# A gated attention block: k of two tiles ahead of q at the outset, and small operations moved between VectorE, ScalarE and GpSimd

## What is computed

```python
xn = layernorm(x)
# s: linear attention and a gated feed-forward part
q, k, v = split(xn @ Wqkv + bqkv)
qp, kp = elu(q) + 1, elu(k) + 1
kv = einsum('bsd,bse->bde', kp, v); num = qp @ kv; den = qp . sum(kp)
x1 = layernorm(xn + num / (den + 1e-6)) * g1 + b1
s = layernorm(x1 + (silu(x1 @ Wg + bg) * (x1 @ Wu + bu)) @ Wd + bd) * g2 + b2
# g: three cycles of a coupling network, and a global network on the mean over the tokens
gf = sigmoid(gelu(gelu(mean(xn) @ gc_w1 + b) @ gc_w2 + b) @ gc_w3 + b)
for 3 cycles:
    tf = sigmoid(gelu(gelu(gelu(out @ w1 + b) @ w2 + b) @ w3 + b) @ w4 + b)
    out = out + (0.1 + range * (0.7 * gf + 0.3 * tf - 0.5) * 2) * twist(out)
return x + s * silu(out)
```

## Time and profile before

| | |
|---|---|
| median of 3 runs | 165.39 us (165.28 to 165.51) |
| the profiled execution, its own time | 163.89 us |
| its span, first to last instruction | 162.1 us |
| TensorE clock granted in it, mean | 0.986 of full |
| busy in the span: PE, DVE, ACT, POOL | 94%, 85%, 81%, 72% |

### The profile page before, as it was taken

One profiled execution on the slowest core, in us unless ns is written; L12 is line 12 of the kernel. 1 busy time (PEld: TensorE's weight loads), 2 busy tenths in 40 slices (PEclk: granted clock), 3 DMA queues, 4 the chain that ended last, 5 costly groups with the idle time before them and its releaser, 6 DMA issues.

```text
span 162.1 us, 3409 instructions
## 1 busy us (share of the span) xinstructions
PE 152.6 (94%) x934; PEld 117.0 (72%) x934; DVE 137.4 (85%) x549; ACT 131.6 (81%) x345; POOL 116.9 (72%) x202
## 2 busy tenths in 40 slices
PE   7889999999999899999999999999999999999940
PEld 7567988888888595545554565788888888888840
DVE  2998699899988998299999968978767999978893
ACT  3989796998999978999999986995648985844950
POOL 0078676699981869995089597379999998896573
PEclk9999999999999999999999999999999999999995
DMA  5997333030230000000000000000000110110113
GB/s 172 256 382 167 65 67 69 0 69 19 50 65 0 2 6 0 0 0 4 0 0 0 4 4 0 0 0 4 0 0 7 60 65 6 65 67 0 65 65 129
DMA packets 11923, 7.83 MB, mean 48 GB/s; under 512 B 8961, under 2 KB 9729, under 8 KB 11905
## 3 DMA queue, kind: packets, MB, share of 16 engines
q1 hardware_dynamic: 11472, 7.28, 15.5%
q10 hardware_dynamic: 432, 0.34, 0.6%
HBM read 3.43 MB, written 2.10 MB: 34 GB/s over the span
## 4 chain that ended last, share of the span: by engine, by line
PE 82%; ACT 7%; issue 3%; DMA 2%; DVE 2%; POOL 2%; POOLq 0%; ACTq 0%; DVEq 0%
PE bank L1074 11%; PE bank L1266 10%; PE bank L1191 7%; PE bank L1255 7%; PE bank L1257 7%; PE bank L1256 7%; PE bank L1203 4%; PE bank L1145 4%; PE bank L1216 4%; PE bank L1132 3%; PE bank L1133 3%; PE bank L1136 3%; PE bank L1156 3%; DMA col<-in_cols 2%; PE bank L1281 2%
## 5 line engine op out<-in xcount | busy, mean ns | idle before, releaser
L515 ACT ACTIVATE pq<-bank,bffn 128x512 f32<-128x512 f32 (+1 forms) x24 | 16.1, 682 | 9.3 <-PE bank L1257 9.3
L271 POOL TENSOR_TENSOR rstd<-ve,minus_half 128x4 f32<-128x4 f32 x21 | 21.2, 1011 | 1.7
L816 DVE SCALAR_TENSOR_TENSOR pq<-bank,bffn,pq 128x512 f32<-128x512 f32 (+1 forms) x24 | 17.6, 739 | 5.2 <-issue 2.4
L1255 PE MATMUL bank<-x_hi,ffn_hi 128*128 128x512 f32 (+1 forms) x48 | 20.5, 427 | 0.0
L1256 PE MATMUL bank<-x_lo,ffn_hi 128*128 128x512 f32 (+1 forms) x48 | 18.9, 395 | 0.0
L1257 PE MATMUL bank<-x_hi,ffn_lo 128*128 128x512 f32 (+1 forms) x48 | 18.9, 394 | 0.0
L1266 PEld LDWEIGHTS bank<-wd,pq 128*128 128x128 f32 x144 | 17.9, 191 | 1.3
L1266 PE MATMUL bank<-wd,pq 128*128 128x128 f32 x144 | 18.0, 274 | 0.0
L455 ACT ACTIVATE q_stage<-bank,col 128x512 f32<-128x512 f32 x24 | 16.0, 677 | 0.1
L269 POOL TENSOR_SCALAR nm<-mv 128x4 f32<-128x4 f32 x21 | 4.7, 223 | 15.4 <-DVE mv L653 15.4
L323 POOL TENSOR_TENSOR ab<-cpl 128x8 f32<-128x8 f32 x4 | 9.7, 2426 | 8.1 <-ACT cpl L487 8.0
(11 more groups left out here) (174 smaller groups left out, 457.7 us busy)
## 6 DMA issues: line engine op xcount, KB each, us to landing
x_tok<-in_x SPq DMA_DIRECT2D x8, 256.0 KB, 6.8
tx_tok<-xn_tok SPq DMA_DIRECT2D x16, 128.0 KB, 2.4
out<-pq SPq DMA_DIRECT2D x6, 256.0 KB, 2.0
r_tok<-in_w_ffn SPq DMA_DIRECT2D x1, 341.0 KB, 6.8
r_tok<-in_w_first SPq DMA_DIRECT2D x1, 320.0 KB, 3.5
out<-pq SPq DMA_DIRECT2D x2, 128.0 KB, 1.7
out<-pq ACTq DMA_DIRECT2D x1, 256.0 KB, 2.2
row<-in_rows SPq DMA_DIRECT2D x1, 192.0 KB, 6.3
```

What stands on the lines that cost most here:

```text
L271: return pool.tensor_tensor(rstd[i][:, b], ve[i][:, b], minus_half[:], ALU.pow)
L816: dve.scalar_tensor_tensor(out=hid[b % 2][0:m, c], in0=up_of(n)[0:m], scalar=bffn[0:m, CHUNKS + c:CHUNKS + c + 1], in1=sg[n % 2][0:m], op0 ...
L1255: pe.matmul(dst[0:m], ffn_hi[:, w], x1_hi[:, b], start=True, stop=False)
```

## The change

1. **PE at the outset.** `project_first` replaces `project_q(0)`, `project_tokens(0)` and `project_tokens(1)`: hi·hi of the two tiles first, then q's, then the rest in the order in which the parts are made. `turn_rows` stands ahead of it.
2. **The halves of batch 0.** The high part of its first half is made by DVE (`hi_first_0`), the second by ACT after the wide cast of `first_hi`. DVE makes the wide `first_lo` before `lo_first(0)` and the narrow one after it, and measures all of batch 2 with its moments before its first `feature_k`; `feature_q(0)` stands after two of them. ACT's `exp_q(0)` stands after tile 1.
3. **ACT to POOL.** `centre_sign` is made by POOL, with a semaphore of its own.
4. **DVE to POOL.** `small_columns` (without `bias_rows`, which DVE now does after norming batch 0) and the sums of x-normed (`join_sums`, two instructions for one) run on POOL in pass b = 7 of its loop, the one ahead of `rstd_of(1, 5)` and the other behind `negate_twisted(3, 4, 5)`.
5. **FFN weights.** Their high part (ACT) and low part (DVE) are made in two halves of 341 columns, after tiles 3 and 6 on ACT, after `feature_k` of tile 6 and after batch 1 on DVE.

```diff
@@ gpsimd @@
+            def join_sums():
+
+                pool.wait_ge(sums_ready, 1)
+                pool.wait_ge(xT_hi_ready, BATCHES - 1)
+                pool.wait_ge(xT_lo_ready, BATCHES)
+                link(pool.tensor_scalar(ctx_sum[:], sum_hi, -OFFSET * SEQ, 0.0, ALU.add, ALU.add))
+                pool.tensor_tensor(ctx_sum[:], ctx_sum[:], sum_lo, ALU.add).then_inc(ctx_ready, 1)
+
+            def small_columns():
...
+                pool.tensor_scalar(gain[:, 1:2], col[:, COL["range"]:COL["range"] + 1], W_TOKEN, 0.0,
+                                   ALU.mult, ALU.add).then_inc(cols_ready, 1)
...
+            pool.tensor_scalar(centre_sign, eye, sign[:, 0:1], minus_mean_sign[:, 0:1], ALU.mult,
+                               ALU.add).then_inc(sign_ready, 1)
...
             for b in range(BATCHES + 2):
                 if b + 2 < BATCHES:
                     norm_x(b + 2)
+                if b == BATCHES - 1:
+                    small_columns()
                 if b >= 2:
                     rstd_of(1, b - 2)
...
                 for done in {6: (0, 1, 2), 7: (3, 4, 5), 8: (6,), 9: (7,)}.get(b, ()):
                     negate_twisted(done)
+                if b == BATCHES - 1:
+                    join_sums()
@@ scalar @@
-            act.activation(centre_sign, eye, ACT.Identity, scale=sign[:, 0:1],
-                           bias=minus_mean_sign[:, 0:1]).then_inc(centre_ready, 1)
...
-            hi_first(0)
-            hi_first(1)
             act.wait_ge(w_ps, 2)
             act.copy(first_hi[:, 0:4 * D], ps_w[:]).then_inc(first_hi_ready, 1)
+            hi_first_1()
             for b in range(BATCHES):
-                exp_q(b)
+                if b >= 1:
+                    exp_q(b)
                 for t in range(TILES):
                     token_tile(TILES * b + t)
-                    if t == (1 if b else 2) and b + 1 < BATCHES:
+                    if b == 0 and t == 1:
+                        exp_q(0)
+                    if t == 1 and b + 1 < BATCHES:
                         hi_x(b + 1)
...
+                    if (b, t) in FFN_AFTER:
+                        split_ffn(FFN_AFTER.index((b, t)))
@@ vector @@
+            def hi_first_0():
+                dve.wait_ge(xT0_ps, 1)
+                dve.tensor_scalar(xT_hi[:, 0, 0:2 * P], ps_xT0[0], OFFSET, 0.0, ALU.add, ALU.add,
+                                  accum_out=half_sums[:, 0, 0:1]).then_inc(xT0_hi_ready, 1)
...
             norm_first(0)
+            bias_rows()
...
-                if b == BATCHES - 1:
-                    dve.wait_ge(sums_ready, 1)
-                    dve.wait_ge(xT_lo_ready, BATCHES)
-                    dve.scalar_tensor_tensor(out=ctx_sum[:], in0=sum_hi, scalar=-OFFSET * SEQ, in1=sum_lo,
-                                             op0=ALU.add, op1=ALU.add).then_inc(ctx_ready, 1)
                 if b >= 1:
                     copy_kv(b - 1)
...
+                if b == 1:
+                    ffn_low(0)
@@ tensor @@
+            def project_first():
...
+                for t in range(2):
+                    pe.matmul(ps_k[t][:], hi[t], first_hi[:, wide], start=True, stop=False)
+                pe.wait_ge(xT0_hi1_ready, 1)
+                pe.matmul(ps_q[:], first_hi[:, wq], xT_hi[:, 0], start=True, stop=False)
...
             transpose_first()
+            turn_rows()
+            project_first()
```

More of the change, by code:

```diff
@@ L643, in measure @@
                 last.then_inc(st_ready[i], 1)
-            def measure_part(b, tiles):
-                for t in tiles:
-                    last = dve.bn_stats(st[0][:, b, t], x_tok[:, b, t])
-                return last
             def moments(i, b, tiles=range(TILES), half=0):
@@ L942, in _ @@
             moments(0, 1)
[L943 to L947 removed]
+            hi_first_0()
             dve.wait_ge(first_hi_ready, 2)
@@ L955, in _ @@
                     add_eps(b - 2)
-                feature_q(b)
+                if b >= 1:
+                    feature_q(b)
                 if b >= 2:
@@ L973, in _ @@
                 if b == 0:
-                    small_columns()
+                    feature_q(0)
+                    lo_x(1)
                 if 1 <= b < BATCHES - 1:
@@ L1106, in transpose_x @@
                 transposes(ps_xT, xn_tok[:, b]).then_inc(xT_ps, 1)
-            def project_q(b):
-                if b == 0:
-                    pe.wait_ge(xT0_hi_ready, 2)
-                    pe.wait_ge(first_ready, 1)
-                else:
-                    pe.wait_ge(xT_hi_ready, b)
-                if b >= 1:
-                    pe.wait_ge(qf_ready, b)
+            def project_first():
+                wq, wide = slice(4 * D, 5 * D), slice(0, 4 * D)
+                hi = [xT_hi[:, 0, t * P:(t + 1) * P] for t in range(2)]
+                lo = [xT_lo[:, 0, t * P:(t + 1) * P] for t in range(2)]
+                pe.wait_ge(xT0_hi_ready, 1)
+                pe.wait_ge(first_hi_ready, 2)
+                for t in range(2):
+                    pe.matmul(ps_k[t][:], hi[t], first_hi[:, wide], start=True, stop=False)
+                pe.wait_ge(xT0_hi1_ready, 1)
+                pe.matmul(ps_q[:], first_hi[:, wq], xT_hi[:, 0], start=True, stop=False)
+                pe.wait_ge(first_ready, 1)
+                for t in range(2):
+                    pe.matmul(ps_k[t][:], hi[t], first_lo[:, wide], start=False, stop=False)
+                pe.wait_ge(xT0_lo_ready, 1)
+                for t in range(2):
+                    pe.matmul(ps_k[t][:], lo[t], first_hi[:, wide], start=False, stop=True).then_inc(k_ps, 1)
+                pe.wait_ge(first_ready, 2)
+                pe.matmul(ps_q[:], first_lo[:, wq], xT_hi[:, 0], start=False, stop=False)
+                pe.wait_ge(xT_lo_ready, 1)
+                pe.matmul(ps_q[:], first_hi[:, wq], xT_lo[:, 0], start=False, stop=True).then_inc(q_ps, 1)
+            def project_q(b):
+                pe.wait_ge(xT_hi_ready, b)
+                pe.wait_ge(qf_ready, b)
                 hi, lo = xT_hi[:, b % 2], xT_lo[:, b % 2]
```

92 lines of the change are left out of this document (44 added, 48 removed).

## The result

The changed kernel takes **170.98 us** (median of 4 runs, 169.91 to 171.69); beside it the kernel before took 165.33 (4 runs, 165.28 to 165.51). The ratio is 1.033, 95% interval 1.028 to 1.039: slower, by 5.65 us. The profiled execution took 171.69, with a span of 169.0 where before had 162.1. It is the longest of the four: their spans are 168.0, 168.3, 168.9 and 169.0.

A forecast was written before the change was run, and what follows sets the result against it. PE (TensorE), busy for 94% of the span, was taken to bound the kernel. Outset +0.2, wait for POOL's join +4.8 and cold clock +1.4 made +6.4 us on a median of 165.39: 171.8 us, range 169.9 to 173.7.

The forecast's parts named there:

- part 3: `join_sums` behind POOL's list in pass 7: PE's `global_layer(0)` waits for it and starts 4.8 us later.
- the outset's 0.2: First microseconds, up to batch 1: the new order was to cost +0.2 us, bounds -0.1 and +0.5.
- part 2: Batch 7 on DVE: without `ctx_sum`, up to 0.91 us, the copy of kv starts 0.8 us earlier.
- A gain of some 0.6 us, if nothing else came up: Batch 7: PE's wait of 0.57 us for DVE's copy of kv would go once `ctx_sum` leaves DVE.
- part 4: TensorE's clock after PE's wait for `ctx_ready`: it falls to half and costs 1.4 us.
- The bounds of 0 and 2.5: Price in us of the halved clock behind PE's wait: nothing at one end, 2.5 at the other.
- the rival's argument: Clock full from the first matmul, so its return may be quick; rival: wait without cold clock, 170.4 us, chance 0.20.
- part 1: The outset: PE's first matmul at about 8.65, `feature_k(0)` 0.2 to 0.3 us later, in all +0.2 us.
- the lower bound: The outset at -0.1 us, where `hi_first_0` is short and PE's earlier start comes through.
- 2.12 us "for five steps that it still has": The outset on DVE: time needed from the aggregation at 7.67 to batch 2's statistics at 9.79, kept in full.
- What it loses or wins before 64 us is carried to the end: PE is busy for all of 89.0 us from 64 to 153 us, so no gap there makes good a loss.
- The sum: Whole kernel: +0.2 + 4.8 + 1.4 = +6.4 us, giving 171.8 us, chance 0.67.

The follow-up runs named there:

- busy run: The changed kernel with 20 unused matmuls of the identity on PE ahead of `global_layer(0)`: 168.49 us, ratio 1.025.
- swap run: The kernel before with POOL's `scale_x1(3)` behind the negations of pass 6 instead of ahead of them: 164.29 us, ratio 0.999.
- the early join alone: The kernel before with only `ctx_sum` moved, as `join_sums` on POOL at the start of pass 7: 164.09 us, ratio 0.997.
- move alone: The kernel before with only `ctx_sum` moved off DVE, onto POOL behind `negate_twisted(3, 4, 5)`: 171.47 us, ratio 1.041.
- wait of 2.85: The changed kernel with `join_sums` between `norm_x1(5)` and `scale_x1(4)` of POOL's pass 7: 167.78 us, ratio 1.018.
- the join first: The changed kernel with only `join_sums` moved, to the start of POOL's pass 7: 164.76 us, ratio 1.003.
- the sum on DVE: The changed kernel with `ctx_sum` back on DVE in its old place: 164.21 us, ratio 0.997.
- the scalars on DVE: The changed kernel with `join_sums` at the start of POOL's pass 7 and POOL's `scalars_2` made by three DVE instructions: 163.78 us, ratio 0.996.

## Why the prediction was right, and which steps failed

- **The place of the loss (part 3)** was right. Forecast: POOL at 57.0, 5.99 us of list, `ctx_ready` 63.5, PE at 63.55. Measured: 57.22, 6.01, about 63.8, 63.93. DVE's moments ended at 57.11 and not at 57.0, and `small_columns`, which "fit into its idle time", filled it to 57.14; the join's second instruction started 0.35 behind the first, not 0.28. Behind its end PE took another 0.15 us. The forecast had added the outset's 0.2 apart, so PE was due at 63.75. That the two agree within 0.2 is in part luck: the profiled execution started late, for a reason that the forecast didn't have (see the outset), and in the busy run, where it didn't, PE came at 63.28.
- **DVE's sum (part 2)** was right on DVE: the copy of kv at 54.33 (forecast 54.3), and the swap run shows the reason. "A gain of some 0.6 us, if nothing else came up" isn't settled: `global_layer(0)` moved by 0.24 in the swap run, and with the early join alone the ratio is worth 0.5 at its middle, with an interval of 0.05 to 0.9.
- **The clock (part 4)**: forecast 1.4, measured 1.65 (changed kernel), 1.09 (move alone) and 1.19 (wait of 2.85). The bounds of 0 and 2.5 held. What I had wrong is the moment of the fall, for which I had one row: less than 2 us after PE's last work at the end of the trace of before, and 1.6 to 3.2 us in these runs. And the rival's argument, a clock that is full from the first matmul on, rested on a column that doesn't show the start (see the end).
- **The outset (part 1)** came out at the forecast number for another reason. Forecast: 8.65, 11.60, 14.5; measured 8.84, 11.54, 14.44. But these rows belong to an execution in which the first matmuls ran slow (1.49 us in L1107). Where they took 0.81, the changed outset gave 11.04 to 11.17 and 13.94 to 14.06 (the join first, the sum on DVE, the busy run, the scalars on DVE), and the old one 11.13 to 11.33 and 14.07 to 14.26 (the kernel before, the move alone, the swap): the new one is some 0.2 ahead at the middle, though the ranges touch. PE's first matmul of the projections came at 8.37 to 8.50 there, 0.2 to 0.35 ahead of the kernel before's 8.72, where I had allowed 0.1. So the case that I had put at the lower bound, a short `hi_first_0` and an earlier start that comes through, is what happened. Two terms failed. `hi_first_0` was to be 0.48; it holds DVE for 0.31. And 2.12 us "for five steps that it still has" contained little waits: the aggregation takes 0.30 of it and the other four steps 1.61, not 1.82. DVE's rows from the run with the join first:

```profile
7.62 0.38 DVE L679 BATCH_NORM_AGGREGATE mv<-st 128x2 f32<-128x6 f32 x4
7.92 0.39 DVE L702 TENSOR_SCALAR_CACHE_REDUCE xT_hi<-bank 128x256 fp32r<-128x256 f32 x1
...
9.84 0.87 DVE L673 BATCH_NORM_STATS2 st<-x_tok 128x6 f32<-128x128 f32 x4
...
11.04 0.25 DVE L732 SCALAR_TENSOR_TENSOR kf<-ek,bank 128x128 f32<-128x128 f32 x1
```

  In sum 0.38 less: +0.27 becomes -0.11. With the join back on DVE and everything else of the change in place the medians say -0.3 (interval -0.9 to 0.0), where I had +0.2.
- **"What it loses or wins before 64 us is carried to the end"** was right for the loss and half right for a win: the 0.68 us of the early join were carried to 97 us and lost at 105.
- **The sum**: +6.4 forecast, +5.65 by the medians, +6.9 by the span of the profiled execution (the longest of its four). Its rows give 5.20 + 1.65, where the forecast had 0.2 + 4.8 and 1.4. For the medians the outset has the other sign: with L1261 at 63.28, as in the busy run, and a clock of 1.09 to 1.65, an estimate from these rows is 5.6 to 6.2. What the three executions without rows lost at each place isn't known. So the place and the kind of the loss were forecast; that the total came within 1 us rests in part on an outset of the wrong sign.

## What to carry to other kernels

When an instruction is moved to a less loaded engine, count the list ahead of its new place to the moment when its result is wanted. This one takes 0.46 us on POOL. Behind 6 us of POOL's work it made the kernel before 4.1% slower; at the head of the same pass it cost nothing. In this kernel, which TensorE bounds, waits of 2.85, 5.19 and 5.24 us cost 1.1 to 1.7 us beyond themselves, because the clock fell, once only when the engine was back at work; a wait of 1.00 cost no clock. And an engine with much idle time was no free place for two-input instructions while VectorE ran a stream of them: look at what waits for them. Last, compare the increase with the increase, not the time with the time: the same kernel before ran in 164.5 or in 165.3 in different jobs.
